# Another order for the opening of a fused FFN and S4 convolution kernel, low halves of weights one step earlier, and another spread of the early down units

## The reference

```python
x = L0_attn_u                                  # 4 x 512 x 512
xn = _layernorm(x, axis=-1)
# S4: kernel K of length 512 from (Lambda, p, q, B, Ct, step), then
y = irfft(rfft(xn, n=1024) * rfft(K, n=1024))[..., :512] + D[0] * xn
# FFN: Wg, Wu (1792 x 512) and Wd (512 x 1792) = NF4_CODE[q] * absmax
h = silu(xn @ Wg.T) * (xn @ Wu.T)
out = x + y + h @ Wd.T
```

## Time and profile before

| | |
|---|---|
| median of 3 runs | 459.99 us (459.29 to 460.63) |
| the profiled execution | 460.08 us, its span 458.3 us, mean granted clock 0.996 |
| TensorE busy | 438.2 us (96%) |
| VectorE busy | 398.4 us (87%) |
| ScalarE busy | 278.8 us (61%) |
| GpSimd busy | 214.6 us (47%) |
| chain that ended last | TensorE 85%, VectorE 6%, ScalarE 2%, transfers 2% |

### The profile page before, as it was taken

How to read it: one execution, slowest core, us unless ns; L and a number is a source line. 1 busy time by engine, 2 the same in 40 slices (tenths; PEclk the granted TensorE clock), 3 DMA queues, 4 the chain that set the end, 5 groups by cost and what they waited for, 6 DMA issues and landing times.

```text
span 458.3 us, 7272 instructions
## 1 busy us (share of the span) xinstructions
PE 438.2 (96%) x2560; PEld 248.8 (54%) x2560; DVE 398.4 (87%) x641; ACT 278.8 (61%) x472; POOL 214.6 (47%) x163
## 2 busy tenths in 40 slices
PE   1879999999999999999999999999999999999997
PEld 1534444443444444434444444466544788888886
DVE  5988979969889798999897879879996999999993
ACT  7868594295877759588684787856032542445340
POOL 2777299547456848669646847778100000000000
PEclk9989999999999999999999999999999999999999
DMA  8543636022315415155222233457691021101111
GB/s 291 172 131 139 144 75 182 1 92 71 138 47 183 161 47 200 54 183 191 63 69 65 61 80 101 111 187 249 193 369 60 1 94 47 46 1 48 47 47 46
DMA packets 34168, 51.41 MB, mean 112 GB/s; under 512 B 13076, under 2 KB 14164, under 8 KB 33364
## 3 DMA queue, kind: packets, MB, share of 16 engines
q1 hardware_dynamic: 34132, 50.95, 35.3%
HBM read 38.03 MB, written 10.81 MB: 107 GB/s over the span
## 4 chain that ended last, share of the span: by engine, by line
PE 85%; DVE 6%; ACT 2%; issue 2%; DMA 2%; POOL 1%; SPq 0%; DVEq 0%; ACTq 0%; POOLq 0%
PE bank L2264 33%; PE bank L2391 21%; PE bank L2109 16%; PE bank L2341 8%; PE bank L2331 6%; ACT work L936 1%; DMA h<-in_x 1%; DVE h L1438 1%; DVE work L1313 1%; DMA work<-in_q_gate 1%; DVE w L1323 1%; DVE work L1309 1%; PE bank L2145 0%; DVE h L1412 0%; POOL h L845 0%
## 5 line engine op out<-in xcount | busy, mean ns | idle before, releaser
L936 ACT ACTIVATE work<-work 128x512 f32<-128x512 f32 (+1 forms) x234 | 130.0, 628 | 11.5 <-POOL work L845 7.8
L845 POOL TENSOR_SCALAR work<-work 128x512 f32<-128x512 int32 x39 | 85.9, 2202 | 64.4 <-DVE work L1309 46.1
L2264 PE MATMUL bank<-h 128*128 128x512 f16 x360 | 81.5, 379 | 0.9 <-ACT bank L1029 0.9
L2109 PE MATMUL bank<-xT,w 128*128 128x512 f16 (+1 forms) x300 | 66.2, 377 | 2.3 <-DVE w L1323 1.1
L2264 PEld LDWEIGHTS bank<-h 128*128 128x128 f16 x360 | 34.9, 98 | 44.0 <-ACT bank L1029 2.4
L2391 PE MATMUL bank<-wd,work 128*128 128x256 f16 x504 | 56.2, 273 | 0.0
L2264 PE MATMUL bank<-xT,w 128*128 128x512 f16 x240 | 55.4, 379 | 0.0
L2391 PEld LDWEIGHTS bank<-wd,work 128*128 128x128 f16 (+1 forms) x504 | 49.3, 98 | 6.0
L2109 PEld LDWEIGHTS bank<-xT,w 128*128 128x128 f16 x300 | 29.4, 99 | 36.8 <-DVE w L1323 2.4
L1250 ACT ACTIVATE work<-h 128x896 f16<-128x896 f32 x30 | 27.9, 942 | 28.4 <-DVE h L2017 18.3
L2391 PE MATMUL bank<-h,work 128*128 128x256 f16 x378 | 42.2, 273 | 0.0
(11 more groups left out here) (181 smaller groups left out, 672.0 us busy)
## 6 DMA issues: line engine op xcount, KB each, us to landing
moved<-h SPq DMA_DIRECT2D x6, 1024.0 KB, 4.9
h<-moved SPq DMA_DIRECT2D x4, 1536.0 KB, 15.5
h<-in_x SPq DMA_DIRECT2D x8, 512.0 KB, 5.4
xT<-in_x SPq DMA_DIRECT2D x16, 256.0 KB, 3.5
out<-xT SPq DMA_DIRECT2D x15, 256.0 KB, 2.1
work<-in_q_gate SPq DMA_DIRECT2D x14, 256.0 KB, 3.6
work<-in_q_up SPq DMA_DIRECT2D x14, 256.0 KB, 2.9
work<-in_am_gate SPq DMA_DIRECT2D x28, 128.0 KB, 3.1
```

Source lines behind the costliest of these rows:

```text
L845: pool.tensor_scalar(chain_room(u, "r"), qs[:, u % 2, :], RIGHT_FROM, RIGHT_FROM, ALU.max, ALU.subtract).then_inc(first_done, 1)
L936: nc.scalar.activation(room, qs[:, u % 2, :] if j == 0 else room, KNEE, scale=scale, bias=bias, alpha=below).then_inc(knee_done, 1)
L2109: mm = nc.tensor.matmul(out_b, weights(k)[:, unit, wl, f, :], xT[:, TPC * c + first:TPC * c + last, xl, f, :], start=(i == 0), stop=(i == ...
L2264: mm = nc.tensor.matmul(out_b, weight(wl, f), token(xl, f), start=(n == 0 and i in (1, 5)), stop=(n == 5), skip_group_check=i not in (1, 5))
```

## The change

It reorders; no computation is added or left out except four warm-up matmuls less (10 and 6 become 8 and 4).

- SyncE: the absmax of unit 0 and the codes of unit 2 are requested ahead of token tiles 4 and 5, the absmax of unit 1 ahead of tiles 6 and 7.
- GpSimd: the norms of token tiles 4 to 7 stand ahead of the first pass of unit 4.
- ScalarE: high half of unit 0 ahead of the first split, the splits of token tiles 4 to 7 in one piece behind the high half of unit 3.
- VectorE, opening: WHOLE and SCALED of unit 0 behind the scales' steps, the steps of unit 2 ahead of the `rstd` steps of the second group, its low half ahead of the last three.
- TensorE: the scales' broadcast ahead of the first transpose; the gate product of tile 1 (unit 2) ahead of the transpose of token tile 4.
- VectorE, everywhere: `(3, 4, 2)` becomes `(2, 3, 4)`. The low half of unit u-1 comes ahead of WHOLE of u, and so the low half of u next behind SCALED of u.
- `window`: `h_mul(n)` follows the first eighth instead of the second.
- `EARLY_IN` becomes (6, 7, 9, 12): tiles 6, 7, 9 and 12 have three units, tiles 8 and 11 two.

```diff
-EARLY_IN = (7, 8, 9, 11)
+EARLY_IN = (6, 7, 9, 12)
...
             first_pass(3)
-            first_pass(4)
             for t in range(TPC, 2 * TPC):
                 norm(t)
+            first_pass(4)
             first_pass(5)
...
                     if u in CHAINED:
-                        i = (3, 4, 2)[i]
+                        i = (2, 3, 4)[i]
...
             moments(4, 8)
+            step(2, WHOLE)
             rstd(1, 0)
             rstd(1, 1)
             rstd(1, 2)
-            scales(9)
+            step(2, SCALED)
             rstd(1, 3)
             rstd(1, 4)
             rstd(1, 5)
-            step(2, WHOLE)
+            scales(9)
             rstd(1, 6)
             rstd(1, 7)
             rstd(1, 8)
-            step(2, SCALED)
+            weight_lo(2)
             rstd(1, 9)
+            scales(10)
             rstd(1, 10)
+            scales(11)
             rstd(1, 11)
-            weight_lo(2)
...
                     h_mul(n + 2)
-                    stage_of(0, 2)
+                    stage_of(0, 1)
                     h_mul(n)
-                    stage_of(2, 4)
+                    stage_of(1, 4)
                     join(0, k, 0)
...
-            warm_up(10)
-            turn(0)
+            warm_up(8)
             pe.wait_ge(one_done, 1)
             pe.wait_ge(sc_done, 7)
             nc.tensor.matmul(bank[0][:, P:P + 6], ones[:], dg3, start=True, stop=True).then_inc(mx_bc, 1)
+            turn(0)
...
+            products(1, (0,))
             turn(4)
-            products(1, (0,))
             turn(5)
```

More of the change, by code:

```diff
@@ L664, in _ @@
             sp.dma_start(amf, am_flat).then_inc(amf_ld, 16)
-            load_x(2)
-            load_x(3)
             load_absmax(0, am_gate[0])
             load_codes(2, q_gate[1])
+            load_x(2)
             load_absmax(1, am_up[0])
+            load_x(3)
             load_codes(3, q_up[1])
@@ L1102, in _ @@
             chain(1, 5, 6)
+            chain(2, 0, 1)
+            weight_hi(0)
             x_hi(0)
-            weight_hi(0)
             x_hi(1)
-            chain(2, 0, 1)
             x_hi(2)
@@ L1113, in _ @@
             weight_hi(2)
-            chain(3, 2, 4)
+            chain(3, 2, 6)
+            silu(0)
+            act.wait_ge(b_mm, 1)
+            nc.scalar.activation(yv[:, 0:2], bank[3][:, 0:2], ACT.Copy).then_inc(b_cp, 1)
+            weight_hi(3)
             x_hi(4)
[L1116 to L1119, removed]
             x_hi(5)
             x_hi(6)
-            act.wait_ge(b_mm, 1)
-            nc.scalar.activation(yv[:, 0:2], bank[3][:, 0:2], ACT.Copy).then_inc(b_cp, 1)
             x_hi(7)
+            chain(4, 0, 1)
             chain(4, 1, 6)
@@ L1568, in _ @@
             rstd(0, 5)
-            step(0, WHOLE)
+            scales(1)
             rstd(0, 6)
@@ L1572, in _ @@
             rstd(0, 8)
-            scales(1)
+            scales(2)
             rstd(0, 9)
-            scales(2)
+            scales(3)
             rstd(0, 10)
-            scales(3)
+            scales(4)
             rstd(0, 11)
-            scales(4)
             dve.wait_ge(id_done, 1)
             scales(5)
+            scales(6)
+            step(0, WHOLE)
+            step(0, SCALED)
             stats(4)
-            scales(6)
-            step(0, SCALED)
-            step(1, WHOLE)
             scales(7)
             scales(8)
+            step(1, WHOLE)
+            weight_lo(0)
             x_lo(0)
-            weight_lo(0)
             x_lo(1)
@@ L1609, in _ @@
             rstd(1, 8)
-            step(2, SCALED)
+            weight_lo(2)
             rstd(1, 9)
+            scales(10)
             rstd(1, 10)
+            scales(11)
             rstd(1, 11)
-            weight_lo(2)
             stats(8)
-            x_lo(4)
-            scales(10)
             step(3, WHOLE)
-            scales(11)
+            scales(12)
             step(3, SCALED)
             h_mul(0)
-            scales(12)
             weight_lo(3)
+            x_lo(4)
             x_lo(5)
@@ L2155, in _ @@
             turn(3)
-            warm_up(6)
+            warm_up(4)
             pe.wait_ge(wlo_done, 1)
```

## The result

The changed kernel takes 476.25 us (median of four runs, 475.58 to 476.56); the kernel before, run beside it, 459.64. The ratio is 1.036 (95%: 1.0333 to 1.0387): 16.6 us slower, where 4.3 us were forecast (a change from 460.08 to 464.3). The profiled execution took 475.58 us with a span of 473.8 and a mean granted clock of 1.000; that is 15.5 us over the profiled execution of before.

What follows compares the result with a forecast made beforehand. TensorE was taken as the bound, busy 438.2 of 458.3 us. From 460.08, the opening's -2.4, old waits' -3.4 and new tile waits' +10.05 gave 464.3 us, range 456 to 468.

Steps and rivals of the forecast that it cites:

- round trip: Three-unit tiles: from WHOLE's start through GpSimd's first pass, cast and high half to the low half, 5.15 us.
- The limit of +8.4: Blocked tile: VectorE's second join must start within 8.4 us of the tile's first x24 row, or TensorE waits.
- x: Start of VectorE's multiplication out of bank 6, counted from a tile's first x24 row; -1.0 us is on time.
- the hand-over: Between tiles: a three-unit tile gives its follower x = +0.37 us, whatever its own x.
- Tile 5: 0.3: New TensorE wait of 0.3 us in tile 5, as TensorE has come forward 1.1 us and VectorE less.
- a tile with two units has room: Two-unit tiles: other work before the low half leaves about 1 us of waiting, which the tile can hold.
- Tiles 12 and 13: New TensorE waits of 0.7 us in tile 12 and 2.1 us in three-unit tile 13, where x = 0.37.
- The opening: Before tile 3: shorter wait, clock staying up, unit 3's product earlier; booked -2.4 us, bounds -3.2 and -0.6.
- The multiplication that now stands ahead of WHOLE helps the copies, not the joins: Earlier multiplication in each tile: removes the 0.95 us copy wait, does nothing for joins; no cost booked.
- A: Rival: VectorE on time at every tile's start, new waits together 6 us, total 460.3 us; chance 0.14.
- B: Rival: low half finds its partner ready, or TensorE doesn't feel it; 454.3 to 455.7 us; chance 0.21.
- C: Rival: the forecast's waits, and the clock falls in the opening; 466.1 us; chance 0.1.

Runs made afterwards that it cites:

- experiment 9: Changed kernel with the new order (2, 3, 4) in two-unit tiles only, (3, 4, 2) in three-unit tiles and behind: 462.23 us, ratio 1.0039.
- experiments 1 and 2: Changed kernel with the old low-half order (3, 4, 2): 460.85 us; kernel before with the new order (2, 3, 4) alone: 471.94 us.
- Experiment 5: Changed kernel with GpSimd's high half ahead of its first pass from unit 13 on: 476.33 us, ratio 1.0369.
- experiment 8: Kernel before with the new opening, and the new order (2, 3, 4) for units below 12 only: 457.95 us, ratio 0.9961.
- experiment 10: Changed kernel with the new order (2, 3, 4) only for units of three-unit tiles and those behind tile 13: 475.3 us, ratio 1.0326.

## Why the prediction was right and wrong

The side was right and so was the mechanism: the low half directly behind SCALED waits for GpSimd, 17 times, and the joins behind it reach TensorE late. The size was 4.3 us where 15.5 came in the trace and 16.6 by the medians, outside the range of 456 to 468. The steps that failed are the size of the round trip, the waits at the end of tiles and behind tile 13, which the sum had at nothing, and the second branch over ScalarE. By the forecast's own steps:

**The limit of +8.4** holds. In tile 6 the second join started at +11.26, 2.86 late, and the tile was 2.96 longer. In tile 7 forecast and measurement are 3.4 and 3.74, and x came out at 0.30 for 0.37, so that the hand-over was right as well. But it was not the only limit. TensorE also waits for joins at a tile's end, which stand behind the last low half. The forecast had no term for these; they came to 1.40 us in tile 5, 1.02 in tile 12 and 1.56 in tile 13:

```profile
145.19 2.87 PE L2263 MATMUL bank<-h,w 128*128 128x512 f16 x12 [1.40 <-DVE h L1411]
```

**The round trip** was taken at 5.15 us and is 5.54 there. I had 1.93 us for the first pass, from one row; it takes 2.43. The group's mean was 2.20 already before. And the row was no fair sample of the new order. There the pass began during a join, and SCALED came 0.4 us later. With the change SCALED stands directly behind WHOLE, so the pass begins with SCALED under way. Before, tile 7 had this order (SCALED at 166.79), and its pass showed the price:

```profile
166.84 2.52 POOL L845 TENSOR_SCALAR work<-work 128x512 f32<-128x512 int32 x1 [6.66 <-DVE work L1309]
```

Then SCALED took 1.10 us instead of 0.69 and x was 0.25 instead of 0. Together these are 1.05 of the 1.2 us by which tile 6 was missed: mis-sized, not misunderstood. Tile 9 repeats it (round trip 5.53, SCALED 1.09): 1.66 for 0.7.

**"Tile 5: 0.3"** and "a tile with two units has room": mis-sized for tile 5, which has 1.83; over the two-unit tiles together experiment 9's trace shows no loss. The wait of 1.40 us at its end is for a join ahead of which both branches were late. The low half had waited 1.47 us, but the step directly ahead of the join could not start before 143.92 in any case, where a step of ScalarE ended whose passes had stood 1.90 us for the first pass. The chain that ended last goes through ScalarE there. ScalarE's branch came late at the tile's start as well: its first row had 0.76 us of idle time behind a step that had waited 1.47 us for ScalarE, and the 0.32 us that tiles 3 and 4 gained are short of the forecast's 1.1 by that much.

```profile
127.30 0.48 DVE L1368 SCALAR_TENSOR_TENSOR h<-h,sc 128x256 f16<-128x256 f32 x1 [1.47 <-ACT h L1057]
...
140.45 0.75 DVE L1322 SCALAR_TENSOR_TENSOR w<-work,sc,w 128x512 f16<-128x512 f32 x1 [1.47 <-POOL w L858]
```

**Tiles 12 and 13** (0.7 and 2.1 forecast, 2.60 and 4.47 measured) were the largest misses. I gave every second unit a wait of 2 us. GpSimd's pass ahead of tile 12's second high half waited for SCALED, not WHOLE, and VectorE then stood 3.09, with the joins of the tile's end behind it. In tile 13 all units are down units and have no sums between SCALED and low half; the small steps there are S4 work, and the wait is 3.32:

```profile
279.50 1.93 POOL L845 TENSOR_SCALAR work<-work 128x512 f32<-128x512 int32 x1 [3.27 <-DVE work L1312]
```

```profile
283.13 0.75 DVE L1322 SCALAR_TENSOR_TENSOR wd<-work,sc,wd 128x512 f16<-128x512 f32 x1 [3.09 <-POOL wd L858]
...
298.33 0.75 DVE L1322 SCALAR_TENSOR_TENSOR wd<-work,sc,wd 128x512 f16<-128x512 f32 x1 [3.32 <-POOL wd L858]
```

**The units behind tile 13** were not in the sum at all. Four of their low halves wait 1.03 to 1.81 us each. The end of the span moved by 1.25 us beyond tile 13. TensorE's idle time there, 0.9 us in its list of waits, is for additions of VectorE (L1959) that stand among these low halves.

**The opening** went as forecast in its steps (30.38 for 30.2, the clock stayed up), with 1.84 for 2.4 in the trace. But part of that was the luck of one execution, and the sum left out that the new order takes longer up to the S4 matmuls; by the ratios of the medians the opening is worth 0.3 to 1.0. "The multiplication that now stands ahead of WHOLE helps the copies, not the joins" left out its cost: 1.5 to 1.9 us beside the old order.

**The rivals.** A falls with tile 6, whose multiplication out of bank 6 starts 0.25 us behind the tile's first row, not on time. Tiles 9 and 12 were on time (x = -1.03 and -1.02) and still cost 1.66 and 2.60 us, where A had 0.7 to 1.0. B falls with the 17 waits and with experiments 1 and 2. C did not happen in the opening: no execution of the kernels with the new opening and the old order had a mean granted clock under 0.999, and neither had any of the changed kernel.

What I missed in kind, and not only in size, is the second branch: WHOLE starts GpSimd's first pass for the low half, and through the same pass ScalarE's chain. I priced only the wait of VectorE. Experiment 5 took most of that wait away and gained nothing.

## What to carry to other kernels

When two engines serve each other in turns, look for the instruction that releases the other engine (here WHOLE) and try it ahead of every wait for that engine; one exchanged step, 0.7 us long, made 15 us here, though what else moved with it was not parted. Price a wait from rows with the same work beside them, or from the mean of the group, not from one row, and then count the units that meet it, through to the program's end. An order that helps at one place (tile 4, 1.1 us) can be used there alone, as experiment 8 does.

## What the runs showed of the hardware

GpSimd's durations depend on what VectorE is doing as they begin. In the traces of the kernel before and of the changed kernel, 25 first passes began 0.04 to 0.08 us behind the start of SCALED and took 2.40 to 2.52 us. The pass took 1.93 us where VectorE stood, and also in the seven rows from tile 3 on in the trace of before that began 0.2 to 0.4 us behind the start of a VectorE step with a bank among its inputs, although SCALED started within each of them; SCALED took 0.72 to 0.84 us there. In experiment 5 one row with VectorE idle (at 144.14, until 147.06), and one that began 0.05 behind a low half:

```profile
144.14 1.93 POOL L845 TENSOR_SCALAR work<-work 128x512 f32<-128x512 int32 x1
...
156.92 2.49 POOL L845 TENSOR_SCALAR work<-work 128x512 f32<-128x512 int32 x1
```

Over the whole program the change moved the contention from one GpSimd instruction to the other: the median first pass went from 2.11 to 2.40 us, since it begins with SCALED under way in 17 of 41 rows now (8 before), and the median high half from 1.82 and 1.90 to 1.57, since VectorE waits for it and stands still. The Trainium skill (GPSIMD Engine Reference, 8. Key points) says that GpSimd shares its SBUF interfaces with VectorE and meets contention where a VectorE instruction has two SBUF inputs; SCALED has two such inputs. The trace agrees in part: 0.5 us on 1.93 where SCALED had begun first, and nothing for the pass where it had not.

The fall of the granted clock in the opening costs less at the end than the trace suggests. The executions of the kernel before with a mean granted clock of 0.996 had medians 0.2, 0.9 and 1.0 us above those with 1.000 in the three comparisons (459.56 and 459.34, 460.26 and 459.32, 459.93 and 458.91), where the slow stretch itself showed 1.7. Why less of it arrives was not tried.

The clock can also fall at the new waits. In experiment 10 it fell behind a wait of 2.07 us in tile 7 (0.67 between 180 and 184 us), and 12 matmuls took 3.83 us instead of 2.75. In the trace of the changed kernel it stayed at 1.00 behind a wait of 2.01 us at the same place.
